# Attention kernel on Trainium2: three bias products removed from the projection loop by shifting normalised rows and weights

## What is computed

```python
Q = layer_norm(x @ Wq + bq, lnq_g, lnq_b)
K = layer_norm(x @ Wk + bk, lnk_g, lnk_b)
V = layer_norm(x @ Wv + bv, lnv_g, lnv_b)
phiQ = tanh(Q @ Wphi_q + bphi_q) + 1
phiK = tanh(K @ Wphi_k + bphi_k) + 1
qg = mean(Qh) / sqrt(D);  alpha = softmax(qg . Kh) * Lq
pKs = phiK * alpha;  KV = pKs^T Vh;  attn = phiQ KV / (phiQ . sum(pKs) + EPS)
attn = layer_norm(attn + gamma * conv(attn), lna_g, lna_b)
s = attn + gelu(attn @ W1 + b1) @ W2 + b2 + x
```

## Time and profile before

| | |
|---|---|
| median of 3 runs | 2357.47 us (2355.94 to 2358.99) |
| profiled execution, its own time | 2365.32 us |
| its span, first to last instruction | 2363.7 us |
| mean granted clock of TensorE | 0.910 |
| PE busy | 1926.7 us (82%) |
| DVE busy | 1495.1 us (63%) |
| POOL busy | 921.7 us (39%) |
| ACT busy | 838.4 us (35%) |

### The profile page before, as it was taken

How to read it: one execution, slowest core, us unless ns; L and a number is a source line. 1 busy time by engine, 2 the same in 40 slices (tenths; PEclk the granted TensorE clock), 3 DMA queues, 4 the chain that set the end, 5 groups by cost and what they waited for, 6 DMA issues and landing times. The chain is left out here.

```text
span 2363.7 us, 46002 instructions
## 1 busy us (share of the span) xinstructions
PE 1926.7 (82%) x12647; PEld 1689.6 (71%) x12648; DVE 1495.1 (63%) x3800; ACT 838.4 (35%) x1983; POOL 921.7 (39%) x1404
## 2 busy tenths in 40 slices
PE   2777777648899688996999999999678898678888
PEld 1555555437599675996999999999555888564887
DVE  2688778745456454564776776776565678565677
ACT  1454444316333253331333333333343233343332
POOL 4344444315545255452321222121362354461453
PEclk9888887769999899998999999999788999788999
DMA  4324223111311113111433333332342022341122
GB/s 142 112 98 147 98 98 115 36 49 50 108 32 57 45 50 104 31 49 63 125 92 108 109 113 102 103 115 73 99 121 83 28 66 70 95 122 54 35 66 68
DMA packets 154783, 196.89 MB, mean 83 GB/s; under 512 B 19913, under 2 KB 140047, under 8 KB 152542
## 3 DMA queue, kind: packets, MB, share of 16 engines
q1 hardware_dynamic: 111598, 124.26, 16.8%
q0 software_dynamic: 16928, 49.43, 6.7%
q10 hardware_dynamic: 26064, 20.99, 2.7%
HBM read 107.34 MB, written 88.21 MB: 83 GB/s over the span
## 5 line engine op out<-in xcount | busy, mean ns | idle before, releaser
L126 PE MATMUL bank<-rows_hi,up_hi 128*128 128x256 f32 x640 | 194.9, 304 | 41.6 <-DVE rows_lo L1769 34.3
L1677 ACT ACTIVATE hid<-bank 128x512 f32<-128x512 f32 x160 | 95.8, 599 | 265.6 <-PE bank L128 222.4
L127 PE MATMUL bank<-rows_lo,up_hi 128*128 128x256 f32 x640 | 188.0, 294 | 0.0
L128 PE MATMUL bank<-rows_hi,up_lo 128*128 128x256 f32 x640 | 187.9, 294 | 0.0
L128 PE MATMUL bank<-down_hi,hid_lo 128*128 128x256 f32 x640 | 181.2, 283 | 0.0
L126 PE MATMUL bank<-down_hi,hid_hi 128*128 128x256 f32 x640 | 181.1, 283 | 0.0
L127 PE MATMUL bank<-down_lo,hid_hi 128*128 128x256 f32 x640 | 181.1, 283 | 0.0
L1786 DVE TENSOR_TENSOR hid_lo<-hid,hid_hi 128x512 fp32r<-128x512 f32 x160 | 126.9, 800 | 71.5 <-ACT hid_hi L1677 69.5
L1085 POOL DMA_INDIRECT job_picked<-h_d,where x128 | 135.0, 1055 | 92.2 <-issue 28.5
L1082 POOL DMA_INDIRECT buf_d<-lt,where x128 | 131.3, 1025 | 93.2 <-issue 69.9
L126 PEld LDWEIGHTS bank<-rows_hi,up_hi 128*128 128x128 f32 x640 | 130.0, 203 | 44.6 <-issue 42.8
(11 more groups left out here) (301 smaller groups left out, 5870.0 us busy)
## 6 DMA issues: line engine op xcount, KB each, us to landing
buf_d<-zeros SPq DMA_DIRECT2D x16, 1280.0 KB, 7.4
rows_in<-buf_d SPq DMA_DIRECT2D x80, 256.0 KB, 3.0
h_d<-h ACTq DMA_DIRECT2D x80, 256.0 KB, 3.2
xa<-in_x SPq DMA_DIRECT2D x20, 512.0 KB, 4.8
x<-in_x SPq DMA_DIRECT2D x16, 512.0 KB, 4.9
after_d<-after SPq DMA_DIRECT2D x16, 512.0 KB, 3.0
ln_d<-ln SPq DMA_DIRECT2D x16, 512.0 KB, 3.3
lt<-ln_d SPq DMA_DIRECT2D x64, 128.0 KB
```

What stands on the lines that cost most here:

```text
L126: pe.matmul(dst, hi, mhi, start=start and i == 0, stop=False)
L127: pe.matmul(dst, hi, mlo, start=False, stop=False)
L128: mm = pe.matmul(dst, lo, mhi, start=False, stop=end)
L1677: act.activation(dst[:, 2 * half:2 * half + 2].rearrange("p f c -> p (f c)"), bank[half][:], ACT.Gelu_apprx_tanh).then_inc(e_hid, 1)
```

## The change

The normalised rows of x, and those of q, k and v, are raised by one. As a normalised row sums to zero over 256 entries, a raised one sums to 256, and a bias (less the column sum of the weights, for the ones that were added) can be put into the weights as one 256th in each row. The bias products of q, k, v (L1272) and of phi of k (L1290) are gone. `inverse_root` gets an argument `lift`: with it, a fifth dependent operation on POOL adds 1 to the bias that ACT applies. It is used for x and for q, k, v, not for the last normalisation. Setup makes the shifted weights: two more groups of products on PE over `wa` (512 and 256 columns), full 128 rows in place of one for `Wphi_k`, four more steps of DVE before PE begins, and scaling and adding on DVE behind PE. ACT makes the high part of `wa` later, behind `wa_shifted`. The row of biases shrinks from 1920 to 896 entries. Uses of q, k, v further on are corrected for the added one within operations that are there already.

```diff
@@ setup: gpsimd, scalar
+                    step(pool.memset(minus[:], -1.0))
...
-                    for i, g in enumerate((lnq, lnk)):
-                        for j in range(HALVES):
-                            step(pool.tensor_scalar(wphi[:, i, j], wphi[:, i, j], g[:, 0, j:j + 1], None, ALU.mult))
+                    for j in range(HALVES):
+                        step(pool.tensor_scalar(wphi[:, 0, j], wphi[:, 0, j], lnq[:, 0, j:j + 1], None, ALU.mult))
...
-                    act.activation(wa_s[0][:], wa[:], ACT.Copy).then_inc(wa_high, 1)
                     act.wait_ge(sums_made, 1)
                     for j in range(HALVES):
                         step(act.activation(w1[:, j], w1[:, j], ACT.Copy, scale=lna[:, 0, j:j + 1]))
+                    act.wait_ge(wa_shifted, 1)
+                    act.activation(wa_s[0][:], wa[:], ACT.Copy).then_inc(wa_high, 1)
@@ setup: tensor
-                    pe.wait_ge(setup_step, 5)
+                    pe.wait_ge(setup_step, 9)
...
-                    for j in range(HALVES):
-                        pe.matmul(bank[3][0:1, 0:E], lnk[:, 1, j:j + 1], wphi[:, 1, j], start=j == 0, stop=j == 1)
+                    for dst, weights, bias, ones in ((bank[3][:, 0:E], [wphi[:, 1, j] for j in range(HALVES)], extra[:, 0:E], bcast_k),
+                                                     (bank[5][:], [wa[:, j, 0:2 * E] for j in range(HALVES)], bqkv[:, 0:2 * E], None),
+                                                     (bank[6][:, 0:E], [wa[:, j, 2 * E:] for j in range(HALVES)], bqkv[:, 2 * E:], None)):
+                        for j in range(HALVES):
+                            pe.matmul(dst, minus[:] if ones is None else ones[:, j], weights[j], start=j == 0, stop=False)
+                        pe.matmul(dst, ones_f[0:1, :], bias, start=False, stop=True)
@@ setup: vector
+                    for j in range(HALVES):
+                        step(dve.tensor_scalar(bcast_k[:, j], ones_f[:], lnk[:, 1, j:j + 1], lnk[:, 0, j:j + 1], ALU.mult, ALU.subtract))
+                    step(dve.tensor_tensor(lnq_shift[:], lnq[:, 1], lnq[:, 0], ALU.subtract))
+                    step(dve.tensor_tensor(lnk_shift[:], lnk[:, 1], lnk[:, 0], ALU.subtract))
...
                     dve.wait_ge(sums_made, 1)
+                    for j in range(HALVES):
+                        step(dve.scalar_tensor_tensor(wa[:, j, 0:2 * E], bank[5][:], 1.0 / E, wa[:, j, 0:2 * E], ALU.mult, ALU.add))
+                        shifted = dve.scalar_tensor_tensor(wa[:, j, 2 * E:], bank[6][:, 0:E], 1.0 / E, wa[:, j, 2 * E:], ALU.mult, ALU.add)
+                    shifted.then_inc(wa_shifted, 1)
+                    step(dve.tensor_scalar(phik_row[:], bank[3][:, 0:E], 1.0 / E, None, ALU.mult))
+                    for j in range(HALVES):
+                        step(dve.scalar_tensor_tensor(wphi[:, 1, j], wphi[:, 1, j], lnk[:, 0, j:j + 1], phik_row[:], ALU.mult, ALU.add))
+                    step(dve.tensor_tensor(bv_row[:], bv_row[:], gv_row[:], ALU.subtract))
...
-                    step(dve.tensor_tensor(brow[:, ROW_PHIK:ROW_PHIK + E], bank[3][0:1, 0:E], extra[:, 0:E], ALU.add))
@@ attend: gpsimd
-                        def inverse_root(n, mv_, step):
+                        def inverse_root(n, mv_, step, lift=None):
...
                             step(pool.tensor_tensor(n[1], n[3], n[0], ALU.mult))
+                            if lift:
+                                step(pool.tensor_scalar(n[1], n[1], lift, None, ALU.add))
...
-                                                 Chain(pool, aq_norm, b * (4 * BT) + 4 * k, pool_passed))
+                                                 Chain(pool, aq_norm, b * (5 * BT) + 5 * k, pool_passed), lift=1.0)
@@ attend: tensor
-                                    for dst, c, width in ((qk_bank[:], ROW_Q, 2 * E), (v_bank[:, 0:E], ROW_V, E)):
-                                        pe.matmul(dst, one_rows[:], brow2[:, c:c + width], start=True, stop=False)
+                                    for dst, c, width in ((qk_bank[:], COL_Q, 2 * E), (v_bank[:, 0:E], COL_V, E)):
                                         mm = split_product(pe, dst, [[w[:, j] for w in xtile[k % 2]] for j in range(HALVES)],
-                                                           [[w[:, j, c:c + width] for w in wa_s] for j in range(HALVES)], start=False)
+                                                           [[w[:, j, c:c + width] for w in wa_s] for j in range(HALVES)])
...
-                                    pe.matmul(bank[1][:, 0:E], one_rows[:], brow2[:, ROW_PHIK:ROW_PHIK + E], start=True, stop=False)
```

More of the change, by code:

```diff
@@ L156, in build @@
         one_rows = sb("one_rows", [P, P], F32R)
-        ROW_Q, ROW_V, ROW_PHIK, ROW_CONV, ROW_OUT, ROW_QKV, ROWS = 0, 512, 768, 1024, 1280, 1536, 1536 + QKV
+        ROW_CONV, ROW_OUT, ROW_QKV, ROWS = 0, 256, 512, 512 + QKV
+        COL_Q, COL_V = 0, 512
         brow2 = sb("brow2", [P, ROWS], F32R)
@@ L180, in build @@
         bphi = sb("bphi", [P, 2, HALVES])
+        lnk_shift = sb("lnk_shift", [P, HALVES])
         phiq_bias = sb("phiq_bias", [P, HALVES])
@@ L206, in build @@
             wa = sb("wa", [P, HALVES, 3 * E], F32, own)
+            lnq_shift = sb("lnq_shift", [P, HALVES], F32, own)
+            minus = sb("minus", [P, P], F32, own)
+            bcast_k = sb("bcast_k", [P, HALVES, P], F32, own)
+            phik_row = sb("phik_row", [P, E], F32, own)
+            bqkv = sb("bqkv", [1, 3 * E], F32, own)
+            wa_shifted = sem("wa_shifted")
             brow = sb("brow", [1, ROWS], F32, own)
@@ L284, in _ @@
                     for i, name in enumerate(("bq", "bk", "bv")):
-                        load(brow[:, i * E:(i + 1) * E], row(a[name]))
+                        load(bqkv[:, i * E:(i + 1) * E], row(a[name]))
                     for i, name in enumerate(("bphi_k", "conv_b", "lna_b", "b2")):
@@ L1069, in norm_x @@
                                 inverse_root([xnorm[g % 2][:, k] for k in range(4)], [xmv[g % 2][:, :, k] for k in range(2)],
[L1070 removed]
+                                             Chain(pool, ax_norm, b * 5 * GROUPS + 5 * g, pool_passed), lift=1.0)
                             def job(j):
@@ L1143, in norm_x @@
                                 if k == 0:
-                                    act.wait_ge(ax_norm, b * 4 * GROUPS + 4 * g + 4)
+                                    act.wait_ge(ax_norm, b * 5 * GROUPS + 5 * g + 5)
                                 act.activation(xnb[:, i], xa[g % 2][:, k], ACT.Identity,
@@ L1160, in _ @@
                                 if 0 <= k < BT:
-                                    act.wait_ge(aq_norm, b * (4 * BT) + 4 * k + 4)
+                                    act.wait_ge(aq_norm, b * (5 * BT) + 5 * k + 5)
                                     if k == 0:
@@ L1289, in _ @@
                                         pe.wait_ge(tk_made, b * BT + k)
-                                    pe.matmul(bank[1][:, 0:E], one_rows[:], brow2[:, ROW_PHIK:ROW_PHIK + E], start=True, stop=False)
                                     for j in range(HALVES):
-                                        mm = pe.matmul(bank[1][:, 0:E], knt[:, j, k * P:(k + 1) * P], wphi[:, 1, j], start=False, stop=j == 1)
+                                        mm = pe.matmul(bank[1][:, 0:E], knt[:, j, k * P:(k + 1) * P], wphi[:, 1, j], start=j == 0, stop=j == 1)
                                     mm.then_inc(phik_done, 1)
@@ L1311, in _ @@
                             for j in range(HALVES):
-                                mm = pe.matmul(bank[1][0:H, 0:1], qheads[:, j], lnk[:, 1, j:j + 1], start=j == 0, stop=j == 1)
+                                mm = pe.matmul(bank[1][0:H, 0:1], qheads[:, j], lnk_shift[:, j:j + 1], start=j == 0, stop=j == 1)
                             mm.then_inc(score_done, 1)
@@ L1482, in _ @@
                                     if k >= 2:
-                                        hold(dve, aq_norm, b * (4 * BT) + 4 * (k - 1), dve_passed)
+                                        hold(dve, aq_norm, b * (5 * BT) + 5 * (k - 1), dve_passed)
                                     for r in range(3):
@@ L1497, in _ @@
                             step(dve.tensor_reduce(qmean[:], qpart[:], AX_X, ALU.add))
-                            step(dve.tensor_scalar(qmean[:], qmean[:], 1.0 / NB, None, ALU.mult))
+                            step(dve.tensor_scalar(qmean[:], qmean[:], 1.0 / NB, -1.0, ALU.mult, ALU.add))
                             step(dve.tensor_tensor(qmean[:], qmean[:], lnq[:, 0], ALU.mult))
```

4 lines of the change are left out of this document (2 added, 2 removed).

## The result

The change takes 2387.69 us (median of 4 runs, 2381.5 to 2395.94), the kernel before 2358.14 (2355.94 to 2358.99): a ratio of 1.0129, 95% interval 1.009 to 1.0168. It is slower by 1.3%, 29.5 us by the medians, where 22.5 were forecast; the range of 2362 to 2396 holds it.

The account below looks back on a forecast made before the run. In attend(0), POOL, PE and a mixed ring lie within half a microsecond; in attend(2) POOL is nearly full. Setup 6.5 + attend(0) 6 + attend(2) 10 = +22.5 us: 2387.8 on the profiled execution, 2380 against the median; range 2362 to 2396.

Parts of the forecast that it names:

- The rival in which POOL's addition hides: In the loops, POOL's addition and PE's gain both hide; only setup is left: 2364 us, chance 0.14.
- the rival with PE in charge: PE sets the pace: attend(0) gains 14.7 us, setup costs 6.5: 2349 us, faster; chance 0.09.
- The rival with everything exposed and contended: All of POOL's added operations show in the time, at contended length: +45 us, 2402; chance 0.17.
- The rule on the shared port: VectorE and GpSimd block each other: added operation nearer 0.65 us in attend(2), its term about 13 instead of 10.
- the loops of `attend(0)`, +3 forecast: Each projection loop of attend(0) grows by 3 us, +6 for two; bounds 0 and 8.4 a pass.
- The rounds through PE gain 0.34 or 0.45 for 0.42 lost and stand still: In attend(0), PE's saved products offset POOL's addition; plain pairs grow +0.1 us on average, 0.6 for six.
- POOL's own ring: POOL's chain over a plain pair of tiles in attend(0): from 7.84 to 8.68 us, against the pair's 8.43 before.
- the loops of `attend(2)`, +5 each forecast: Each projection loop of attend(2) grows by 5 us, +10 for two; bounds 0 and 12 a pass.
- the prediction's own sign: It calls itself wrong if a pass's loop is shorter than before, or setup grows under 2 or over 12 us.
- There is no PE ring to shorten: In attend(2), products removed from PE were taken to give no gain; only POOL's addition was counted.
- setup, +6.5 forecast: Setup grows by 1.0 (PE's later start) + 3.2 (PE's stream) + 2.3 (DVE behind PE) us; bounds +2 and +12.
- I expect the full level for its last 5 us ... and for most of the 7.0 us of L344's narrow products: In setup, PE's clock rises during the new 10 us stream, saving 2.4 and 2.8 us: PE net +3.2.

Follow-up runs that it names:

- e1: Kernel before plus a fifth dependent POOL operation (adds 0.0) for x and for q, k, v; all bias products stay: 2379.1 us, 1.0092.
- e6: The change with the lift moved off POOL into existing ACT and DVE copies of x and k, q and v not raised: 2362.0 us, 1.0028 of before.
- e8: The change with a second added dependent operation on POOL (adds 0.0): 2410.8 us, 1.0228 of the kernel before.
- e10: Kernel before with 78 filler products on PE into an unused bank while the weights load: 2351.9 us, 0.9984.
- e5: The change run again unaltered, for a second profile: 2381.9 us, 1.0108 of the kernel before.
- e2: Kernel before without the bias products of q, k, v and phi of k, those biases left out: 2350.3 us, 0.9978.
- e3: The change with products by a tile of zeros put back where the bias products stood: 2374.8 us, 1.0077 of the kernel before.
- e11: The change with three products into an unused bank ahead of PE's wait for the next tile of x: 2376.9 us, 1.0107 of before.
- e7: As e6, with the shift of Wq, Wk, Wv done early, while the other weights load: 2350.9 us, 0.9974 of the kernel before.
- e9: As e7, with 38 filler products on PE ahead of its other setup products: 2350.9 us, 0.9976 of the kernel before.
- e4: The change with only x lifted; q, k, v not lifted, phi of k keeps its bias product: 2354.9 us, 1.0007 of before.

## Why the prediction was right or wrong

**Right: the sign, and what carries it.** The forecast was slower by 22.5 us, through one dependent operation on POOL; measured, 29.5. e1's ratio alone is worth 22 us, that of e6, without the operation, 7. The operation costs what was taken: 0.24 + 0.20 us, 0.43. The rival in which POOL's addition hides falls by e1, the rival with PE in charge by e2. The rival with everything exposed and contended, 2402, was 14 us off; but e8 shows that a second operation is mostly exposed, at 6.4 to 6.9 of 8.6 us a loop.

**The rule on the shared port**, as the prediction applied it, would have made the operation cost nearer 0.65 us in `attend(2)`. L1089's median there is 0.248 against 0.234 in `attend(0)`, its maximum 0.501: contention now and then, and the term of 13 it gave did not come. e10 does agree with the rule of the Trainium skill, SBUF — State Buffer (SBUF: two separate sides), that the loser waits out the other's whole instruction: DVE's 2.97 us operation, which reads SBUF alone, ends with POOL's. The five DVE operations just before it ran beside the same POOL operation at 0.16 to 0.55 us each; each of them reads a PSUM bank.

**Mis-sized: the loops of `attend(0)`, +3 forecast, +5.4 and +10.0 measured (e5: +6.2 and +9.9).** The step "The rounds through PE gain 0.34 or 0.45 for 0.42 lost and stand still" holds where the clock stays at its full level. The measure is the stretch from POOL's first operation of the ninth tile of a loop to that of the fifteenth, three plain pairs. It takes 26.7 us in the kernel before and in e10; 28.0 in e1, with the operation alone; 25.6 in e2, with the columns out alone; and 26.7 again in the first loop of e5, the one loop of the change's four in which the clock is full all through it. POOL's timeline there (e5):

```profile
584.21 0.23 POOL L1084 TENSOR_SCALAR qnorm<-qmv 128x3 f32<-128x3 f32 x1 [0.67 <-POOL xnorm L1089]
...
590.08 0.29 POOL L1084 TENSOR_SCALAR qnorm<-qmv 128x3 f32<-128x3 f32 x1
...
592.90 0.23 POOL L1084 TENSOR_SCALAR qnorm<-qmv 128x3 f32<-128x3 f32 x1 [0.35 <-POOL qnorm L1089]
```

This plain pair, 5.87 + 2.82 = 8.69 us, has no wait for DVE in it: it is POOL's own ring, forecast at 8.68. That is also why the second leg is never e2's 2.60 in the change: POOL's five operations and the gap behind them take 2.82, so of the 0.35 us that the columns give back, 0.13 can be used in such a pair.

What the sum left out is the clock. It took the full level for granted behind the first tile. Busy time of the same stretch by window, e5's first loop, then the change's two loops:

```profile
584.20:610.90 26.70, 20.71 (x122) 17.43 (x120) 12.09 (x47) 14.50 (x49) 16.98 (x36) 1.00 0.11 41
```

```profile
585.70:613.10 27.40, 22.22 (x122) 18.76 (x120) 12.22 (x47) 15.33 (x51) 17.07 (x37) 0.94 0.12 40
890.80:920.40 29.60, 24.15 (x123) 20.17 (x122) 12.27 (x47) 15.99 (x52) 16.96 (x36) 0.88 0.12 41
```

With one stretch at the low level it takes 27.4 us, with two 29.6, for the same work; where the clock is full, runs with the same code in the loop agree there within 0.05 us. Adding up the shortest of the change's four starts, pairs and ends of a loop, those with low clock behind the start left out, gives 92.4 us, an estimate: +4 on the 88.5 of the second loop before, which has no low clock there either. So the terms at full clock were some 1 us short, in the two pairs with x (1.4 and 1.5 more, 1.26 forecast) and behind the last pair (+0.7, nothing forecast); the other 3 to 6 us of a loop go with the low clock. e1, e3 and e11 have less of it, and second loops of 96.1, 96.2 and 95.5 where the change has 98.5 and 98.4. The prediction named a fall of the clock as a risk, but in `attend(2)`; there it reads 0.86 for 0.85, and in the second loop of `attend(0)` 0.91 for 1.00.

**Mis-sized the other way: the loops of `attend(2)`, +5 each forecast, +1.4 and −0.5 measured.** By the prediction's own sign, a loop shorter than before means that it was wrong; the second loop is shorter, by less than the spread. POOL's term was right: e1 stands 4.5 us above the mean of two profiles without the operation (before and e10), and the change 4.7 above e6, e7 and e9. What failed is "There is no PE ring to shorten", which booked nothing for the 0.46 us a tile that leave PE. The ten loops of e2, e4, e6, e7 and e9, which have neither the columns of q, k and v nor the operation on them, have a mean of 118.1 us (115.7 to 119.8), the four of before and e10 one of 120.4 (118.3 to 122.6); with the operation, the change's four have 122.2, the four of e1 and e3 124.1. Either way the columns are worth some 2 us a loop, which is about the spread of single loops. The working also set 5.35 us, which ends with the second gather, beside 6.35, which runs to the next tile's start; to the same point the slower tile takes 5.92 (2105.48 to 2111.40). A quarter of idle time on PE did not mean that PE's work is free. That this is because the clock is low for some 30% of the stretch, so that PE's work weighs more there, is likely but not shown.

**Mis-sized: setup, +6.5 forecast, +10.1 measured**, inside its bounds of 2 and 12. PE's start was +1.6 (1.0 forecast), DVE's tail +1.4 (2.3), PE's stream +7.2 (3.2). The step that failed is "I expect the full level for its last 5 us ... and for most of the 7.0 us of L344's narrow products". The clock rose 11.7 us after PE's first product and fell again under the narrow ones. In e3 it came early and stayed, and the setup grew by 3.4 us only. What picks between the two is open: e3 and e11 have it early, the change in both profiles and e8 late, and one memset ahead of the loads is all that differs in their setup code; of the kernels whose setup code differs by more, e4 has it early and e6 late. The Trainium skill, TensorE: Matmul & The Clock Gate (Part 1), has the clock doubled after sustained activity; e10, whose filler products begin at 1.18 us and whose own all run at the full level from 22.75, agrees, but it does not tell the two cases here apart.

That the forecast came so near the result is thus partly luck: two misses in `attend(0)` and setup (some 9 and 4 us) were partly met by one in `attend(2)` (9 us the other way).

## What to carry to other kernels

Before work is moved off one engine onto another, find the chain that is without waits: here a 0.43 us operation, 80 times in POOL's chain, cost 22 us, and 29 us of PE time bought 5. Then ask what the longer waits do to the clock of the engine that got less work. A constant can be added inside an operation that already runs (the bias of a copy, a third operand), and with the setup's new products moved beside the loads the same algebra then pays: e7 is 0.9974 of the kernel before, the change 1.0129. What a removed product is worth is read by taking the products out alone; busy shares of PE said "much" for `attend(0)` and "nothing" for `attend(2)`, and it was 1 to 2 us a loop in both.

## What the runs showed of the hardware that I had not expected

Taking work from PE can lower its clock. With the columns out and the operation in, PE waits for ACT for 16.3 us in 11 places of the second loop instead of 9.0 in 7, and the granted clock is 0.91 there; with the columns back (e3) it is 1.00, and without the operation (e6) 0.98. Neither alone did it in these runs; e1 and e2 have one or two stretches of low clock in a loop after its first 12 us, the change 3 and 5 in both its profiles. The row of e8, with a longer chain on POOL still, is 0.92:

```profile
852.10:935.20 83.10, 59.44 (x312) 49.83 (x311) 34.58 (x134) 42.71 (x138) 51.10 (x118) 0.92 0.12 43
```

In the first loop the change is no longer than e1, e3 and e11 (95.4 and 96.2 against 95.9 to 96.1), in the second by 2.2 to 3 us. That is not far from the spread of a loop, but it came in both profiles. Waits of PE in the change, 848 to 928 us:

```profile
PE bank L126 <- ACT vn L1199: 16.3, 11, 3.0
```

And a float32 stream on PE may stay at the low level far longer than the stream that starts a loop: 14 us in the setup of the kernel before, with 32 narrow products in 6.99 us, against 3.73 in e10 at the full level. The level is told here from the pace of the products; the page's clock row starts at 9 tenths, and the trace of the kernel before holds no record of the clock ahead of 68 us.
